# A graph attention kernel: rows without neighbours in two batches, one worked out during the stream

## The chip, the cores and the metric

One core of one Trainium2 chip. The metric is the device time of one execution in microseconds (us), median of three runs, lower is better. The profile comes from one further execution with the hardware profiler. Engines: TensorE (PE), VectorE (DVE), ScalarE (ACT), GpSimd (POOL) and SyncE (SP, which issues DMAs).

## What is computed

```python
N, D = (8192, 128)                       # x: (8192, 128) fp32, adj: (8192, 8192) int32, attn: (256, 1)
h = jnp.maximum(_layernorm(x, axis=-1), 0.0)
s_i = h @ attn[:d]
s_j = h @ attn[d:]
e = jax.nn.leaky_relu(s_i + s_j.T, negative_slope=0.2)
e = e + jnp.where(adj > 0, jnp.float32(0.0), neg_inf)     # neg_inf = -1e9
alpha = jax.nn.softmax(e, axis=1)
return x + alpha @ h
```

Each entry of `adj` is 1 with probability 0.000488, so a row has 4 neighbours on average and 169 of the 8,192 rows have none. In such a row every score has the same -1e9 added, and the softmax goes over all 8,192 columns. At -1e9 fp32 has steps of 64, so for most such rows all scores round to one value and the result is the mean of `h`; where the row's `s_i` is so large that some scores may round to another step (the kernel calls the tile entries "wild"), the whole row has to be worked out.

## The kernel before, in words

Row `64 p + t` lies in partition `p` and tile `t`; there are 64 tiles of 128 rows, taken two at a time as 32 pairs, and each tile is loaded in two halves of 128 x 4096 integers (2 MB).

**Setup.** `x` stays in `x_all`, `h` with its scores in `h_all` (128 x 64 x 132). `h` also goes to a table in DRAM, for gathers.

**Stream**, step `p` of 32. SP loads the halves into the four slots of `adj_ring` (`load_pair`, L352), each as soon as ScalarE has turned the slot's last content into signs (`sign_tile`, L527). TensorE packs the signs of a tile into words that hold column numbers (`pack_tile`, L1147; three buffers `words`), VectorE takes the largest words (`max_tile`, L650), decodes column numbers of up to 8 neighbours per row in 12 slots a pair (`find_pair`, L663) and marks rows with more neighbours than fit (`flag_pair`, L706); TensorE ranks these (`rank_pair`, L1166), VectorE makes one-hot rows of the ranks (`key_pair`, L738), TensorE lists their words (`list_pair`, L1174). GpSimd gathers the neighbours' rows of `h`, 12 indirect DMAs per pair (`gather_pair`, L450). Two steps later VectorE scores them (`score_pair`, L748), ScalarE takes exp (`exp_pair`, L547), VectorE sums 16 weighted rows onto `x` (`add_pair`, L773), and SP stores them. Per segment of 8 pairs the listed ("deep") rows are redone with 16 neighbours: `find_deep`, 17 gathers (`gather_m`, L460), `score_deep`, `add_deep` and an indirect store (`store_m`, L475). Segment 3 is done after the stream.

**Rows without neighbours**, all in the last step (p = 31), in 128 places for the whole matrix. `lone_mark` (L887) finds up to 4 per partition among the 64 tiles; TensorE ranks them (L1210 to L1215); `lone_compact` (L900) makes one-hot rows; TensorE spreads `s_i` and the row numbers over the places (L1217 to L1225); `lone_bounds` (L930) works out ids and maxima; `lone_part` (L946), four parts of 16 tiles, writes the scores of 128 places against 2,048 columns with three instructions of 2,048 elements per partition into slots 2 and 3 of `adj_ring`; ScalarE takes exp (L578 to L581); TensorE multiplies by `h_all` (L1226 to L1231, 128 matmuls); `lone_end` (L961) divides and adds `x`, which GpSimd has gathered (L493 to L498); GpSimd stores (L500 to L504). Behind `lone_part` on VectorE stand `add_pair` and `score_pair` of the last three pairs, then the sizing of the far loop, `score_deep(3)` (L1071), `add_deep(3)` and `lone_end`. GpSimd's order behind the pairs is `store_m(2)`, the gather of x, `gather_m(3)` with 17 gathers, `store_m(3)`, the store of the places.

**Far loop.** Rows that fit nowhere go through a loop over tiles and 32 pieces of 256 columns on all engines. It turns at least once. Rows without neighbours that find no place are such rows (`lost`).

Order between engines is by semaphores: `wait_ge` on an engine holds everything behind it on that engine.

## Time and profile before

| | us |
|---|---|
| median of 3 runs (lowest, highest) | 868.03 (866.70, 868.43) |
| the profiled execution: time | 867.93 |
| the profiled execution: span of the core | 866.2 |
| busy in the span: PE, DVE, ACT, POOL | 460.1, 569.3, 521.1, 571.0 |
| DMA queues moved | 301.56 MB, mean 348 GB/s |
| share of the chain that ended last: DMA, DVE, "issue" | 69%, 11%, 13% |

The span is what the profile shows of the core; 1.7 us lie around it. Busy shares are means over a stream and a tail that have different limits, so a stage has to be read by its own rows. The chain of waits is followed back from the last instruction to whatever released each step. "Idle before" in a timeline is the time an engine stood still before the instruction, with what released it; `issue` means nothing in the profile did. Several VectorE instructions overlap by some 0.1 us, so a group is better timed from its start to the next one's start.

### The profile page before, as it was taken

How to read it: one execution, taken by the hardware profiler on the slowest of the kernel's cores; microseconds unless marked ns; L12 is line 12 of the kernel's file. 1: busy time of each engine (PE TensorE's matmuls, PEld its weight loads, DVE VectorE, ACT ScalarE, POOL GpSimd, SP SyncE). 2: the span in 40 equal slices, each digit the busy share in tenths (PEclk: the TensorE clock that was granted, in tenths of full speed). 3: DMA queues.
4: the chain of work that ended last, by engine and by line, in shares of the span. 5: the costliest groups of instructions: out<-in, count | busy, mean ns of one | idle time of the engine just before them, and what ended most of it. 6: DMA issues, size and time to landing. Idle time of an engine off the chain costs nothing.

```text
span 866.2 us, 7055 instructions
## 1 busy us (share of the span) xinstructions
PE 460.1 (53%) x1605; PEld 191.2 (22%) x1633; DVE 569.3 (66%) x2273; ACT 521.1 (60%) x357; POOL 571.0 (66%) x527
## 2 busy tenths in 40 slices
PE   0665465655555665566555656556566455623601
PEld 0332122221212222122222222222222122213600
DVE  7998266565676666656766465568656566668981
ACT  1895676666676666676666666667666677600200
POOL 6631776666567777666678777667776867758810
PEclk9998777676886678776788686876767788665955
DMA  8799999999999999999999999999999999511000
GB/s 346 286 382 404 399 406 409 410 410 410 406 408 409 410 408 409 405 410 411 404 406 410 408 411 406 414 405 412 404 405 403 408 391 404 196 25 27 18 16 14
DMA packets 39515, 301.56 MB, mean 348 GB/s; under 512 B 10611, under 2 KB 16948, under 8 KB 22065
## 3 DMA queue, kind: packets, MB, share of 16 engines
q1 hardware_dynamic: 24176, 277.23, 79.1%
q0 software_dynamic: 15296, 23.88, 8.0%
q8 instruction: 13, 0.21, 0.1%
q14 instruction: 30, 0.24, 0.1%
HBM read 303.63 MB, written 8.91 MB: 361 GB/s over the span
## 4 chain that ended last, share of the span: by engine, by line
DMA 69%; issue 13%; DVE 11%; ACT 5%; PE 1%; DVEq 0%; POOL 0%; SPq 0%; ACTq 0%; POOLq 0%
DMA adj_ring<-in_adj_dram 68%; ACT sign_ring L533 3%; DVE mixed L797 1%; DVE one_hot L609 1%; ACT h_all L544 1%; DVE adj_ring L954 1%; DVE adj_ring L958 1%; DVE adj_ring L949 1%; DVE mixed_m L879 1%; DMA x_all<-in_x_dram 1%; PE words L1160 0%; DVE codes L616 0%; DVE codes L619 0%; PE words L1220 0%; PE words L1223 0%
## 5 line engine op out<-in xcount | busy, mean ns | idle before, releaser
L533 ACT ACTIVATE sign_ring<-adj_ring,half_neg 128x4096 bf16<-128x4096 int32 x128 | 474.6, 3708 | 226.4 <-DMA adj_ring<-in_adj_dram 226.4
L455 POOL DMA_INDIRECT near<-h_table,near_id x384 | 443.8, 1156 | 198.9 <-issue 109.2
L1160 PE MATMUL words<-sign_ring,pack_w 128*128 128x512 bf16 x1004 | 357.2, 516 | 282.3 <-ACT sign_ring L533 279.6
L656 DVE MAX8 cand<-words 128x8 f32<-128x256 f32 x256 | 91.1, 418 | 223.9 <-PE words L1160 223.8
L1160 PEld LDWEIGHTS words<-sign_ring,pack_w 128*128 128x128 bf16 x1024 | 114.1, 121 | 516.7 <-ACT sign_ring L533 357.2
L797 DVE SCALAR_TENSOR_TENSOR mixed<-near,weight_n,mixed 128x128 f32<-128x128 f32 x448 | 120.3, 345 | 0.0
L470 POOL DMA_INDIRECT near_m<-h_table,id_m x64 | 79.1, 1235 | 19.5 <-issue 19.5
L1152 PE MATMUL words<-place,place_w 128*128 128x512 bf16 x120 | 47.2, 478 | 1.1 <-issue 1.0
L1142 PE MATMUL listing<-h_all 128*1 128x128 f32 x128 | 20.4, 335 | 33.7 <-ACT h_all L544 33.7
L581 ACT ACTIVATE adj_ring<-adj_ring 128x2048 f32<-128x2048 f32 x4 | 7.6, 1910 | 49.8 <-DVE adj_ring L958 49.8
L1179 PEld LDWEIGHTS listing<-cand,one_hot 128*128 128x128 f32 x128 | 28.1, 271 | 12.6 <-issue 6.5
L1229 PE MATMUL words<-h_all,adj_ring 128*128 128x129 f32 x128 | 18.8, 316 | 15.7 <-ACT adj_ring L581 15.7
L1179 PE MATMUL listing<-cand,one_hot 128*128 128x34 f32 x128 | 23.3, 317 | 2.5 <-DVE one_hot L745 2.5
L533 ACT ACTIVATION_READ_ACCUMULATOR sign_ring<-adj_ring,half_neg 128x1 f32 x128 | 23.9, 186 | 0.0
L434 POOL TENSOR_SCALAR h_all<-x_all,codes 128x128 f32<-128x128 f32 x16 | 13.0, 825 | 14.5 <-DVE codes L628 14.5
L1142 PEld LDWEIGHTS listing<-h_all 128*1 128x1 f32 x128 | 12.8, 102 | 41.4 <-issue 27.1
L672 DVE TENSOR_TENSOR codes<-cand_i,code_mask 128x512 int32<-128x512 int32 x32 | 21.9, 684 | 0.0
L1229 PEld LDWEIGHTS words<-h_all,adj_ring 128*128 128x128 f32 x128 | 18.1, 229 | 16.4 <-ACT adj_ring L581 16.4
L642 DVE TENSOR_TENSOR near<-h_all,mixed 128x2048 f32<-128x2048 f32 x8 | 21.5, 2683 | 0.0
L797 DVE SCALAR_TENSOR_TENSOR mixed<-near,weight_n,x_all 128x128 f32<-128x128 f32 x64 | 19.8, 350 | 1.1
L544 ACT ACTIVATE h_all<-x_all,codes 128x128 f32<-128x128 f32 x48 | 18.8, 480 | 0.2 <-DVE codes L628 0.2
L647 DVE TENSOR_REDUCE h_all<-near 128x16 f32<-128x2048 f32 x8 | 18.3, 2288 | 0.3
(213 smaller groups left out, 431.4 us busy)
## 6 DMA issues: line engine op xcount, KB each, us to landing
adj_ring<-in_adj_dram SPq DMA_DIRECT2D x128, 2048.0 KB, 18.9
near<-h_table,near_id POOLq DMA_INDIRECT x384, 6.4
h_table<-h_all POOLq DMA_DIRECT2D x4, 1056.0 KB, 12.2
x_all<-in_x_dram SPq DMA_DIRECT2D x4, 1024.0 KB, 9.6
out_dram<-mixed SPq DMA_DIRECT2D x32, 128.0 KB, 18.5
near_m<-h_table,id_m POOLq DMA_INDIRECT x64, 6.2
adj_ring<-h_table SPq DMA_DIRECT2D x1, 132.0 KB, 3.1
mixed<-in_L_gnn_attn_dram SPq DMA_DIRECT2D x1, 128.0 KB, 6.5
```

Of the source, the lines that this page charges most:

```text
L455: pool.indirect_dma_start(out=near[:, p % RING, k, :], out_offset=None, in_=table, in_offset=bass.IndirectOffsetOnAxis(ap=near_id[:, p % I ...
L470: pool.indirect_dma_start(out=near_m[:, k, :], out_offset=None, in_=table, in_offset=bass.IndirectOffsetOnAxis(ap=id_m[:, k:k + 1], axis=0 ...
L533: nc.scalar.activation(sign_ring[:, n % 4, :], adj_ring[:, n % 4, :], ACT.Sign, bias=half_neg[:, :], accum_out=degree[:, t, h:h + 1]).then ...
L544: nc.scalar.activation(h_all[:, t, 0:D], x_all[:, t, :], ACT.Relu, bias=shift[:, t:t + 1], scale=rstd[:, t:t + 1]).then_inc(h_ready, 1)
L656: last = nc.vector.max(out=cand[:, p % 2, t % 2, 8 * q:8 * q + 8], in_=words[t % 3][:, q * PART:(q + 1) * PART])
L672: nc.vector.tensor_tensor(codes[:, :, :, :].rearrange("p a w c -> p (a w) c"), cand_i[:, :, :].rearrange("p a w -> p (a w)").unsqueeze(2). ...
L797: ins = nc.vector.scalar_tensor_tensor(acc, near[:, e, slot, 0:D], weight_n[:, a * own + k:a * own + k + 1], base, ALU.mult, ALU.add)
L1142: last = nc.tensor.matmul(listing[0:1, 0:D], h_all[:, t, ONE:ONE + 1], h_all[:, t, 0:D], start=(t == 0), stop=(t == TILES - 1))
L1152: nc.tensor.matmul(at[:, k * BANK:(k + 1) * BANK], place_w[:, :], place[:, k * BANK:(k + 1) * BANK], start=True, stop=False)
L1160: last = nc.tensor.matmul(at[:, k * BANK:(k + 1) * BANK], pack_w[:, c, :], sign_ring[:, n % 4, o + k * BANK:o + (k + 1) * BANK], start=Fal ...
L1179: last = nc.tensor.matmul(listing[:, 0:REC], one_hot[:, p % 2, a, :], cand[:, p % 2, a, :], start=(p % SEG == 0 and a == 0), stop=(p % SEG ...
L1229: last = nc.tensor.matmul(lone_sum, lone_p[:, t * P:(t + 1) * P], h_all[:, t, 0:ONE + 1], start=(t == 0), stop=(t == TILES - 1))
```

## The change

The rows without neighbours are taken in two batches. Batch 0 is tiles 0 to 45 (the first 23 pairs), with 64 places; batch 1 is tiles 46 to 63 (the last nine pairs), with 32 places. Each has its own semaphores and buffers; the functions take the batch `b`.

- **Batch 0** runs in the stream, its VectorE steps at the end of a step of the pair loop (`lone_step`): mark in step 22, compaction in 23, bounds and part 0 in 24, parts 1 to 3 in 25 to 27 (each 16 tiles x 64 places), sums of the parts (`lone_add`) in 27 to 30, the end in 30. Its buffers lie in the `x_all` tiles 0 to 39, which `add_pair` has used up. TensorE, ScalarE and GpSimd do their steps in between. TensorE's results lie in the bank `rank`, which `rank_pair` writes too, so `rank_pair` gets waits for VectorE's reads.
- **Batch 1** takes the place of the old code: two parts of 32 tiles x 32 places.
- GpSimd stores batch 0 between `store_m(2)` and the gather of x for batch 1.
- The far loop gets its `x` by a DMA of SP, since `x_all` has been overwritten.
- Unused partitions of the ids are set aside by two more memsets; one more instruction in the bounds drops the ids of a batch that has more rows than places.

```diff
-    LC = 4
-    LT = TILES // LC
+    EARLY = 23
+    FIRST_STEP = EARLY + 1
+    LAST = 1
+    LONE_CAP = (64, 32)
+    LONE_PARTS = (4, 2)
+    LONE_TILES = (slice(0, 2 * EARLY), slice(2 * EARLY, TILES))
+    LONE_BUFS = 3
+    DEAD = 40
...
+        early_x = x_all[:, 0:DEAD, :].rearrange("p t d -> p (t d)")
...
-        lone_p = adj_ring[:, 2:4, :].rearrange("p h w -> p (h w)").bitcast(fp32)
+        lone_p = [[early(lone_size[0], fp32) for _ in range(LONE_BUFS)],
+                  [adj_ring[:, 2, c * lone_size[1]:(c + 1) * lone_size[1]].bitcast(fp32)
+                   for c in range(LONE_PARTS[1])]]
...
-        lone_rank = words[1][:, BANK:BANK + LONE]
-        lone_rec = words[1][:, BANK + 16:BANK + 17]
-        lone_spread = words[0][:, BANK:BANK + P]
-        lone_sum = words[2][:, BANK:BANK + ONE + 1]
+        lone_rank = [rank[:, 72:72 + LONE], words[1][:, BANK:BANK + LONE]]
+        lone_rec = [rank[0:LONE_CAP[0], 76:77], words[1][0:LONE_CAP[1], BANK + 16:BANK + 17]]
+        lone_spread = [rank[:, 448:448 + LONE_CAP[0]], words[0][:, BANK:BANK + LONE_CAP[1]]]
+        lone_sum = [rank[0:LONE_CAP[0], 260:260 + ONE + 1], words[2][0:LONE_CAP[1], BANK:BANK + ONE + 1]]
...
+                    sp.wait_ge(far_free, DC * t + c + 1)
+                    sp.sem_inc(sp_passed, 1)
+                    sp.dma_start(far_x, x_t[:, ds(t, 1), :].rearrange("p o d -> p (o d)")).then_inc(far_x_in, 16)
...
             for p in range(PAIRS):
                 gather_pair(p)
+                if p == FIRST_STEP + 2:
+                    load_lone(0)
...
             store_m(SEGS - 2)
-            pool.wait_ge(lone_id_ready, 1)
-            pool.indirect_dma_start(
-                out=lone_x, out_offset=None, in_=x,
...
+            store_lone(0)
+            load_lone(LAST)
             gather_m(SEGS - 1, range(0, DEEP))
             store_m(SEGS - 1)
...
+            store_lone(LAST)
...
+            def exp_lone(b, c):
+                part = lone_p[b][c % len(lone_p[b])]
+                act.wait_ge(lone_masked[b], c + 1)
+                nc.scalar.activation(part, part, ACT.Exp).then_inc(lone_exp[b], 1)
...
+                if FIRST_STEP <= p - 1 < FIRST_STEP + LONE_PARTS[0]:
+                    exp_lone(0, p - 1 - FIRST_STEP)
...
+            def lone_mark(b):
+                ts = LONE_TILES[b]
+                dve.wait_ge(flags_ready, ts.stop // 2)
                 dve.wait_ge(bounds_ready, 5)
+                if b == 0:
+                    dve.wait_ge(pair_mixed, DEAD // 2)
+                nc.vector.memset(lone_x[b], 0.0).then_inc(lone[b], 1)
+                nc.vector.memset(lone_out[b], 0.0).then_inc(lone[b], 1)
+                nc.vector.memset(lone_id[b], 2 * N).then_inc(lone[b], 1)
...
+            def lone_part(b, c):
+                lt = TILES // LONE_PARTS[b]
+                ts = slice(c * lt, (c + 1) * lt)
+                form = [P, lt, LONE_CAP[b]]
+                part = lone_p[b][c % len(lone_p[b])]
+                tiled = part.rearrange("p (t e) -> p t e", e=LONE_CAP[b])
+                if c >= len(lone_p[b]):
+                    dve.wait_ge(lone_summed[b], c - len(lone_p[b]) + 1)
+                nc.vector.tensor_tensor(tiled, lone_si_b[b].unsqueeze(1).broadcast_to(form),
+                                        h_all[:, ts, SJ].unsqueeze(2).broadcast_to(form), ALU.add) \
+                    .then_inc(lone_masking[b], 1)
...
+            def lone_add(c):
...
+                dve.wait_ge(lone_summed[0], c + 1)
+                if c == 0:
+                    nc.vector.tensor_copy(acc, lone_sum[0]).then_inc(lone[0], 1)
+                else:
+                    dve.wait_ge(lone[0], n + c)
+                    nc.vector.tensor_tensor(acc, acc, lone_sum[0], ALU.add).then_inc(lone[0], 1)
...
+            def lone_step(p):
+                if p == FIRST_STEP - 2:
+                    lone_mark(0)
+                if p == FIRST_STEP - 1:
+                    lone_compact(0)
+                if p == FIRST_STEP:
+                    lone_bounds(0)
+                if 0 <= p - FIRST_STEP < LONE_PARTS[0]:
+                    lone_part(0, p - FIRST_STEP)
+                if 0 <= p - FIRST_STEP - 3 < LONE_PARTS[0]:
+                    lone_add(p - FIRST_STEP - 3)
+                if p == FIRST_STEP + 3 + LONE_PARTS[0] - 1:
+                    lone_end(0)
...
                 if m >= 0 and p % SEG == DEEP_MIX and p < PAIRS - 1:
                     add_deep(m)
+                lone_step(p)
...
-                                                   x_all[:, ds(t, 1), :].rearrange("p o d -> p (o d)"),
+                    dve.wait_ge(far_x_in, 16 * DC * t + 16 * c + 16)
+                    dve.sem_inc(dve_passed, 1)
+                    nc.vector.scalar_tensor_tensor(far_out, far_acc[:, 0:D], far_inv[:, 0:1], far_x,
                                                    ALU.mult, ALU.add).then_inc(far_out_ready, 1)
...
+                if p >= FIRST_STEP - 1:
+                    pe.wait_ge(lone[0], LONE_MARK + LONE_HOT)
+                if p >= FIRST_STEP:
+                    pe.wait_ge(lone_id_ready[0], 1)
+                    pe.wait_ge(lone[0], LONE_MARK + LONE_HOT + LONE_IDS)
+                if 0 <= p - FIRST_STEP - 3 < LONE_PARTS[0]:
+                    pe.wait_ge(lone[0], LONE_MARK + LONE_HOT + LONE_IDS + p - FIRST_STEP - 2)
                 nc.tensor.matmul(place_at, before[:, :], flag[:, e, :], start=True, stop=False)
...
                 list_pair(p - 1)
+                if p == FIRST_STEP - 1:
+                    lone_ranks(0)
+                if p == FIRST_STEP:
+                    lone_spreads(0)
+                c = p - FIRST_STEP - 2
+                if 0 <= c < LONE_PARTS[0]:
+                    lone_matmuls(0, c)
```

`lone_ranks`, `lone_spreads` and `lone_matmuls` are TensorE's old lines (L1210 to L1231) for a batch; a `lone_matmuls(0, c)` is 16 matmuls with 64 places as its weights and a sum of its own, `lone_matmuls(1, c)` is 32 with 32 places.

## Rows read from the trace of the kernel before

**Rows 1.** The page: DMA share in 40 slices, issues of the adjacency with landing.

```profile
DMA  8799999999999999999999999999999999511000
...
adj_ring<-in_adj_dram SPq DMA_DIRECT2D x128, 2048.0 KB, 18.9
```

**Rows 2.** The chain that ended last: start us, us, what.

```profile
736.36 18.88 DMA adj_ring<-in_adj_dram
...
779.93 0.53 DVE adj_ring L905
...
787.41 2.21 DVE adj_ring L949
...
815.42 4.29 DVE mixed L797 x16
...
821.85 4.29 DVE mixed L797 x16
```

**Rows 3.** Groups by line and form, VectorE, 100 to 867 us: count, busy, mean ns.

```profile
L958 DVE SCALAR_TENSOR_TENSOR adj_ring<-adj_ring 128x2048 f32<-128x2048 f32 x4 | 9.2, 2293 | 0.2
...
L905 DVE TENSOR_TENSOR adj_ring<-h_all,adj_ring 128x256 f32<-128x256 f32 x1 | 0.6, 597 | 0.0
...
L763 DVE SCALAR_TENSOR_TENSOR leaky<-valid_score 128x16 f32<-128x16 f32 x32 | 5.7, 178 | 1.1
```

**Rows 4.** Timeline of VectorE, the end: start us, us, instruction, idle before.

```profile
786.20 0.29 DVE L933 COPY adj_ring<-words 128x128 f32<-128x128 f32 x1 [2.92 <-PE words L1223]
...
814.81 0.16 DVE L779 TENSOR_REDUCE total<-weight 128x2 f32<-128x16 f32 x1
...
835.01 0.23 DVE L847 TENSOR_SCALAR score_m<-near_m,si_m 128x16 f32<-128x16 f32 x1
...
847.96 0.17 DVE L1091 TENSOR_SCALAR adj_ring<-adj_ring 128x2 f32<-128x2 f32 x1 [5.90 <-POOLq L511]
...
858.31 0.35 DVE L1128 SCALAR_TENSOR_TENSOR adj_ring<-adj_ring,x_all 128x128 f32<-128x128 f32 x1 [0.24 <-DVE adj_ring L1126]
```

**Rows 5.** Timeline of TensorE, 700 to 867 us.

```profile
782.60 2.07 PE L1220 MATMUL words<-adj_ring 128*128 128x128 f32 x8 [10.83 <-DVE adj_ring L919]
...
810.04 5.48 PE L1229 MATMUL words<-h_all,adj_ring 128*128 128x129 f32 x32 [3.02 <-ACT adj_ring L581]
```

**Rows 6.** Timeline of GpSimd, 700 to 867 us.

```profile
767.69 1.00 POOL L455 DMA_INDIRECT near<-h_table,near_id  x1 [5.39 <-DVE near_id L701]
...
787.15 1.02 POOL L494 DMA_INDIRECT adj_ring<-in_x_dram,adj_ring  x1 [1.23 <-DVE adj_ring L938]
...
788.48 2.01 POOL L465 DMA_INDIRECT x_m<-in_x_dram,row_m  x1 [0.31 <-issue]
...
816.09 1.09 POOL L470 DMA_INDIRECT near_m<-h_table,id_m  x1 [0.30 <-issue]
...
817.48 3.12 POOL L470 DMA_INDIRECT near_m<-h_table,id_m  x1 [0.30 <-issue]
...
823.64 1.01 POOL L470 DMA_INDIRECT near_m<-h_table,id_m  x1 [0.30 <-issue]
```

**Rows 7.** DMA issues of 816 to 832 us and of 842 to 858 us, median landing.

```profile
near_m<-h_table,id_m POOLq DMA_INDIRECT x5, 2.3
...
adj_ring<-in_adj_dram SPq DMA_DIRECT2D x1, 128.0 KB, 6.0
```

**Rows 8.** Busy time per stretch: pair 23, then pair 24.

```profile
578.00:601.00 23.00, 14.21 (x45) 5.46 (x45) 18.27 (x79) 15.51 (x11) 14.48 (x11) 0.73 1.01 410
...
601.00:624.00 23.00, 14.45 (x43) 5.18 (x43) 16.24 (x75) 15.31 (x9) 15.84 (x16) 0.65 1.01 406
```

**Rows 9.** Timeline of VectorE in step 25, then of ScalarE in the same step.

```profile
617.34 1.42 DVE L656 MAX8 cand<-words 128x8 f32<-128x256 f32 x4
...
628.29 0.20 ACT L549 ACTIVATE weight<-below 128x16 f32<-128x16 f32 x1
...
630.34 3.71 ACT L533 ACTIVATE sign_ring<-adj_ring,half_neg 128x4096 bf16<-128x4096 int32 x1 [1.85 <-DMA adj_ring<-in_adj_dram]
```

More of the change, by code:

```diff
@@ new lines, in graph_attention_kernel @@
+        homes = (early, end)
+        widths = [ts.stop - ts.start for ts in LONE_TILES]
+        lost = early(TILES, fp32)
+        lonely = [home(w, fp32) for home, w in zip(homes, widths)]
+        lone_at = [home(w, fp32) for home, w in zip(homes, widths)]
+        lone_top = [home(8, fp32) for home in homes]
+        lone_here = [home(4, bf16) for home in homes]
+        lone_key, lone_si = ([home(LONE, fp32) for home in homes] for _ in range(2))
+        lone_eq, lone_pick = ([home(LONE * w, fp32) for home, w in zip(homes, widths)] for _ in range(2))
@@ L210, in graph_attention_kernel @@
+        lone_x, lone_out = ([home(D, fp32) for home in homes] for _ in range(2))
+        lone_acc = early(ONE + 1, fp32)
+        far_x = end(D, fp32)
+        lone_size = [TILES // n * e for n, e in zip(LONE_PARTS, LONE_CAP)]
+        lone_p = [[early(lone_size[0], fp32) for _ in range(LONE_BUFS)],
+                  [adj_ring[:, 2, c * lone_size[1]:(c + 1) * lone_size[1]].bitcast(fp32)
+                   for c in range(LONE_PARTS[1])]]
+        assert early_taken[0] <= DEAD * D
         far_h = end(DB * COLS, fp32).rearrange("p (k c) -> p k c", k=DB)
@@ L333, in graph_attention_kernel @@
         SIZING = 11
-        LONE_MARK = 4
+        LONE_MARK = 6
         LONE_HOT = 8
-        LONE_IDS = 5
+        LONE_IDS = 6
         FAR_STEPS = 11
@@ L577, in _ @@
             exp_step(PAIRS - 1)
-            for c in range(LC):
-                part = lone_p[:, c * LT * P:(c + 1) * LT * P]
-                act.wait_ge(lone_masked, c + 1)
-                nc.scalar.activation(part, part, ACT.Exp).then_inc(lone_exp, 1)
+            for c in range(LONE_PARTS[LAST]):
+                exp_lone(LAST, c)
             exp_pair(PAIRS - 2)
```

295 lines of the change are left out of this document (161 added, 134 removed).

## The prediction

> **What bounds the kernel now.** I read the page first. For the first 85% of the span the DMA engines are busy in every slice but the first two at 90% or more; in the last 15% they are almost idle [rows 1]. So there are two stages with different limits: a stream in which the adjacency matrix comes in, and a tail of about 110 us after the last half tile. The chain of waits says the same: it goes from load to load up to 755 us, and then through VectorE. The long links of the tail are the masking of the rows without neighbours, from 787.4 to 814.8 us [rows 2, 4]. The timeline of VectorE shows that it waits for almost nothing between 786.2 and 842 us [rows 4]: the tail is a list of VectorE work, and what leaves that list comes off the end, until something else is late. The timeline of GpSimd shows the candidate: it issues 17 gathers (x_m and 16 of near_m) from 788.48 to 824.65 us, and `score_deep(3)` on VectorE at 835.01 needs all of them [rows 4, 6]. The last lands by 825.9 [rows 6, 7]: GpSimd has 9 us to spare there, no more. In the stream, VectorE is busy 18.3 and 16.2 of 23 us in the two fullest steps [rows 8].
>
> **The change, part by part, in the tail.**
>
> Masking. Before: four parts of 16 tiles x 128 places, three instructions of 2,048 elements each, 12 in all, 27.4 us (814.81 - 787.41) [rows 2, 4]. After: two parts of 32 tiles x 32 places, 6 instructions of 1,024. A row of 2,048 takes 2.293 us and one of 16 takes 0.178 [rows 3], so 1.04 ns per element and 1,024 take about 1.23 us; with the overlap seen before (27.4 / 12 = 2.28) the step is 1.22. Six make 7.3 us: **20.1 us less**.
>
> Compaction works on 4 x 18 elements, not 4 x 64. L905 takes 0.597 us for 256 [rows 3]; between it and the 16-element row, 72 elements give about 0.28. Two such and one reduction save some 0.85 us; four one-hot rows of 32 columns, not 128, save about 0.3. Two more memsets add 0.2. TensorE's spreading, for which VectorE waited 2.92 us out of 3.6 [rows 4, 5], has 32 columns or 32 weights, not 128. No row has that shape; between nothing saved and half (1.8 us) I take 1.2, nearer to half, since both operands shrink to a quarter. The bounds have one instruction more and smaller ones: zero, within 0.3. Together 2.2 us. So VectorE's list is **22.3 us** shorter: masking ends at 792.5, and the sizing that ended at 835.0 ends at 812.7.
>
> GpSimd then. Its list before the 17 gathers: `store_m(2)`, which must have ended at 785.9, since 1.23 us of waiting lead up to 787.15; then, new, `store_lone(0)`, whose data has been ready since step 30: 1.02 + 0.30 us. It takes the place of that wait [rows 6], so the `load_lone` comes at 787.5 and x_m at 788.8. Undisturbed, an indirect gather takes 1.00 us and 0.30 to the next: 17 are 22.2 us, or a last start at 809.7. But it isn't undisturbed. While the 2.29 us instructions of the masking run, one gather goes through per VectorE instruction and takes 2.01 us [rows 6]. With instructions of 1.22 us the same lockstep holds for at most the 3 gathers before 792.5: x_m until the step that ends at 789.9, plus 0.9: 1 us lost there and 0.1 to 1 later; I take 1.1. Then the 16 accumulations of a pair, 4.29 us in a row, from 815.42 and from 821.85: a gather that starts 0.67 us into them takes 1.09 us, one 1.79 in takes 1.01, and one 2.06 in takes 3.12 and ends 0.9 after the last of them [rows 2, 6]. Laying the new gathers against the pairs' accumulations (793.1 to 797.4, 799.5 to 803.8, 805.9 to 810.2) one gather in each is held, and costs 0.9, 1.0 and 1.2 us; the short delays before them add some 0.1 each, the lockstep some more where it falls otherwise: 5.7 us in all. The last gather starts at 815.4 and lands 2.3 us later [rows 7]: 817.7. VectorE, ready at 812.7, now **waits about 5 us** for it, where it waited for nothing.
>
> So `score_deep(3)` moves from 835.0 to 817.7, **17.3 us**. What follows it (7 us of deep work, stores, the far loop's one turn) is the same list. New in it: the load of x for the far loop. SP issues it once `far_free` is raised, at which VectorE's own wait ends (847.96), and it is used at 858.31 [rows 4]; the adjacency piece next to it took 6.0 us [rows 7]. It lands 4 us ahead: zero. If that cover were gone, it would cost 6 at most.
> TensorE still runs 128 matmuls for the last batch, four groups like the 5.48 us one [rows 5]: at worst 22 us from 790, done by 812 and needed first for the count of severe rows at 811. What that delays lies under the 5 us wait.
>
> **In the stream.** Batch 0 adds to VectorE: mark 1.1 (seven short instructions, an estimate from the 0.178 us row), compaction 3.4 (2.7 from L905 to where TensorE starts, and four short ones) [rows 2, 5], bounds 1.3 (1.21 before, from 786.20 to 787.41), four parts of 16 x 64 = 1,024 elements with three instructions each, 14.6, sums and end 1.6: 22.0 us in nine steps. Worst are step 23 (18.3 + 3.4 of 23) and step 24 (16.2 + 1.3 + 3.7 of 23) [rows 8]. TensorE, which in `rank_pair` now waits for the end of VectorE's step, not its middle, may lose 7 to 10 us at pairs 23 and 24 (an estimate: the 4.3 us of accumulations and the work added), but it stands idle before each half tile: of each 23 us it is busy 14 [rows 8]. I carry the delay on: `max_tile(50)`, at 617.34 before, comes at 625.4, and the scores of pair 23 end at 628.3. Exactly then ScalarE wants them, at 628.29, and it has 1.85 us before its next half tile [rows 9]. And behind ScalarE stands a second cushion: a load lands 18.9 us after its issue, though 2 MB at 406 GB/s are 5.2 us of transfer [rows 1, 8], so ScalarE may be 13 us late before the DMA engines run dry. The stream costs **nothing** by this; in the range I allow 0 to 3 us. GpSimd is later by up to 5 us in steps 24 to 29 (held gathers, one more load) and has 5.39 us idle before pair 31 [rows 6].
>
> **Sum**: own span 866.2 - 17.3 = 848.9. The profiled execution took 867.93 us in all, 0.1 below the median of 868.03; the sum for that is 850.7, and I say 851.
>
> On the hold of GpSimd the Trainium skill (SBUF — State Buffer, Who interferes with whom) has a rule of its own: a VectorE instruction with two SBUF inputs and a GpSimd instruction that reads SBUF exclude each other, for one whole instruction. The masking rows agree. The 3.12 us row doesn't: the accumulations are some 0.27 us each (4.29 / 16) and it was held for all that were left. By the rule alone the three held gathers would cost 0.3 each, and the gain would be 19 us.
>
> **The rivals.**
> (a) GpSimd isn't late: short instructions let gathers through, and VectorE's list is all. For it: gathers of 1.0 us beside accumulations; 17 at 1.3 land at 812. Against it: a 2.0 to 3.1 us gather in nearly every accumulation. Gain 22.3: **845.7**.
> (b) GpSimd is held far more, with 2.32 us per gather for all 17 as beside the masking: last start 788.8 + 16 x 2.32 = 825.9, landed 828.2, gain 6.8: **861**. Against it: the masking is over by 792.5.
> (c) The other side: the backlog of VectorE reaches the loads. The place is the exp of pair 23 to 26 on ScalarE, queued ahead of the sign of a half tile, whose end lets SP issue the next load. It decides if ScalarE falls more than 13 us behind; then, at worst, all 22.0 us lengthen the stream: 868.0 + 22.0 - 17.3 = **873**, slower. Against it: 628.3 against 628.29, and steps 25 to 30 win time back. A part of it, 3 to 12 us, would give 854 to 863.
> (d) It doesn't do what it says: if more than 64 rows of the first batch, or 32 of the last, need a place, they fall to the far loop, whose single turn lasts some 12 us and which would turn 32 times for every tile: hundreds of us. Counted from the reference's inputs, 41 rows need one of the 64 places and 21 one of the 32, so this is as good as excluded.
>
> **How the numbers follow.** Forecast (GpSimd ends last, 847.5 to 855): 0.68. (a) 0.13. (b) 0.06. (c) in part 0.07, in full 0.04; (d) and the unnamed 0.02. The range 845 to 857 takes in (a), the unknown terms (1.8 us of spreading, 1 to 3 us of lockstep, 0 to 3 us in the stream) and leaves out some 0.15. A difference of 0.2%, 1.7 us, is what can be told from none: faster 0.94, within 0.01, slower 0.05.
>
> **What would show it.** Right: the chain of the end goes through GpSimd's near_m gathers and their landing; VectorE idles 3 to 8 us before `score_deep(3)`; six masking instructions of 1.2 us; gathers of 2 to 3 us only in the accumulations; the last adjacency load lands within 1 us of before. Wrong: no idle there (a), more than 3 us later ends of the stream (c), a wait for `far_x` before the last multiplication, or more than one turn of the far loop (d).

## The result, and the profile after

| | before | after |
|---|---|---|
| median of 4 runs (lowest, highest), us | 867.37 (866.57, 868.43) | 855.60 (854.06, 856.33) |
| the profiled execution: time, span, us | 867.93, 866.2 | 855.79, 854.0 |
| ratio after to before, 95% interval | | 0.9861 [0.9842, 0.9880] |

The change takes 11.8 us off. The forecast was 17; the time lies inside the range. In this document's tables the median counts all executions, while the ratio leaves out slow ones, those more than 1.5% above the fastest of the same kernel; counted in full, `no_batch0` would stand at 0.980 and `reads_first` at 0.989, and the other ratios within 0.003 of what is given.

Between the two profiled spans the difference of 12.2 us splits like this (each piece is the difference of two times in the traces):

| piece | before | after | difference |
|---|---|---|---|
| start to the sign of half tile 114 of 128 | 682.07 | 678.62 | -3.4 |
| from there to the flags of the last pair (L735, L783) | 86.6 | 93.2 | **+6.6** |
| flags to `score_deep(3)` | 66.3 | 47.3 | **-19.0** |
| `score_deep(3)` to the last store's start | 24.5 | 24.5 | 0 |
| last store's start to the end of the span | 6.7 | 10.4 | **+3.7** |

Of the first piece, 2.8 us are there at the first half tile (32.8 us after the start, not 35.6), long before batch 0 starts. In all the traces of this case the first sign starts at 32.8 to 33.0 or at 35.6 to 35.9 us, with batch 0 and without, so this belongs to the execution and not to the change. The two bold plus signs are what the forecast didn't have.

The page of the changed kernel, the slices and the chain (they answer to [rows 1]):

```profile
DMA  8899999999999999999999999999999999911100
GB/s 344 336 379 391 404 408 409 410 411 412 409 411 411 408 409 406 410 410 413 412 408 407 413 409 404 412 410 408 401 405 405 401 363 376 372 35 31 40 22 4
...
DMA 61%; issue 14%; DVE 8%; POOL 6%; PE 5%; ACT 4%; DVEq 0%; SPq 0%; POOLq 0%; ACTq 0%
```

Slices 33 to 35, at 363 to 376 GB/s, were not there before: the DMA engines were no longer fed quite fast enough. And TensorE, 1% of the chain before, now has 5%.

**The tail** did what the forecast said. VectorE's timeline (start, duration, line, tile, idle before; it answers to [rows 4]):

```profile
787.20 0.19 DVE L990 COPY adj_ring<-words 128x32 f32<-128x32 f32 x1 [1.81 <-PE words L1304]
...
788.02 1.22 DVE L1016 TENSOR_TENSOR adj_ring<-adj_ring,h_all 128x1024 f32<-128x1024 f32 x1
789.27 1.22 DVE L1020 SCALAR_TENSOR_TENSOR adj_ring<-adj_ring 128x1024 f32<-128x1024 f32 x1
...
794.25 1.23 DVE L1024 SCALAR_TENSOR_TENSOR adj_ring<-adj_ring 128x1024 f32<-128x1024 f32 x1
795.40 0.16 DVE L827 TENSOR_REDUCE total<-weight 128x2 f32<-128x16 f32 x1
...
815.57 0.15 DVE L1166 TENSOR_SCALAR adj_ring<-adj_ring 128x1 int32<-128x1 f32 x1
819.16 0.23 DVE L895 TENSOR_SCALAR score_m<-near_m,si_m 128x16 f32<-128x16 f32 x1 [3.43 <-DMA near_m<-h_table,id_m]
...
842.45 0.35 DVE L1227 SCALAR_TENSOR_TENSOR adj_ring<-adj_ring 128x128 f32<-128x128 f32 x1 [0.26 <-DVE adj_ring L1223]
```

Six masking instructions take 7.4 us (795.40 - 788.02); they were 27.4. From the flags (771.83) to L1166 VectorE needs 43.7 us, 22.5 less than the 66.2 of before (768.71 to 834.94). Then it waits 3.43 us for a gather. The last multiplication (L1227) waits only 0.26 us, for VectorE itself, so the load of `far_x` costs nothing.

GpSimd's timeline beside it (answers to [rows 6]):

```profile
787.87 1.03 POOL L510 DMA_INDIRECT out_dram<-mixed_m,row_m  x1 [0.30 <-issue]
789.20 1.00 POOL L526 DMA_INDIRECT out_dram<-x_all  x1 [0.30 <-issue]
790.51 1.04 POOL L517 DMA_INDIRECT adj_ring<-in_x_dram,adj_ring  x1 [0.30 <-issue]
791.85 2.01 POOL L496 DMA_INDIRECT x_m<-in_x_dram,row_m  x1 [0.31 <-issue]
794.16 0.99 POOL L501 DMA_INDIRECT near_m<-h_table,id_m  x1 [0.30 <-issue]
...
798.05 3.11 POOL L501 DMA_INDIRECT near_m<-h_table,id_m  x1 [0.30 <-issue]
...
809.29 1.10 POOL L501 DMA_INDIRECT near_m<-h_table,id_m  x1 [0.30 <-issue]
...
812.01 2.06 POOL L501 DMA_INDIRECT near_m<-h_table,id_m  x1 [0.30 <-issue]
...
816.97 0.99 POOL L501 DMA_INDIRECT near_m<-h_table,id_m  x1 [0.31 <-issue]
```

Of the 17 gathers four are longer than 1.01 us (2.01, 3.11, 1.10, 2.06); they lose 4.3 us together. The last starts at 816.97, lands 2.16 later by the chain, and releases L895.

**The stream** is where the forecast failed. TensorE's timeline of the lone matmuls of batch 0 (L1317) and of `rank_pair` (L1276):

```profile
684.27 6.26 PE L1317 MATMUL rank<-h_all,x_all 128*64 128x129 f32 x32 [14.77 <-DVE x_all L1032]
...
709.81 5.46 PE L1317 MATMUL rank<-h_all,x_all 128*64 128x129 f32 x32 [10.98 <-DVE x_all L1035]
...
734.54 5.04 PE L1317 MATMUL rank<-h_all,x_all 128*64 128x129 f32 x32 [10.98 <-DVE x_all L1035]
...
758.86 0.16 PE L1276 MATMUL rank<-flag,before 128*128 128x2 bf16 x1 [6.65 <-DVE x_all L1035]
```

L1032 and L1035 are the two forms of `lone_add`, at the very end of VectorE's step. The code of `lone_matmuls(0, c)` says why: for c > 0 it waits for `lone_add(c - 1)`, because both use the same sums in PSUM. In the order of the instructions TensorE reaches `lone_matmuls(0, c)` in step 26 + c, behind `list_pair`; `lone_add(c - 1)` stands at the end of VectorE's step 26 + c, behind `max_tile(2p+1)`, the finding, the flags and `add_pair`. So TensorE stands still until VectorE's `add_pair` and the work behind it are over, three times, 36.7 us together (14.77 + 10.98 + 10.98), with the next tile's packing queued behind.

How the delay reaches the loads: ScalarE's timeline, its sign of the first half tile after each of these waits:

```profile
692.89 3.71 ACT L576 ACTIVATE sign_ring<-adj_ring,half_neg 128x4096 bf16<-128x4096 int32 x1 [4.12 <-PE words L1258]
...
717.63 3.71 ACT L576 ACTIVATE sign_ring<-adj_ring,half_neg 128x4096 bf16<-128x4096 int32 x1 [6.67 <-PE words L1258]
...
741.95 3.71 ACT L576 ACTIVATE sign_ring<-adj_ring,half_neg 128x4096 bf16<-128x4096 int32 x1 [8.54 <-PE words L1258]
```

ScalarE has no slot to write signs to, because TensorE hasn't packed the old ones; so it frees the slots of the loads later, and SP issues the loads later. The chain of waits goes the same way (start, duration, engine, tile, line):

```profile
705.18 3.84 DVE mixed L845 x15
709.12 0.34 DVE mixed L845
709.81 5.46 PE rank L1317 x32
715.42 0.38 PE words L1250
715.80 3.45 PE words L1258 x16
719.28 0.45 PE words L1250 x2
719.74 3.47 PE words L1258 x16
723.23 1.44 DVE cand L704 x4
```

It is a ring: `add_pair`, lone matmuls, packing, `max_tile`, `add_pair`. From 661.68 us on no load of the adjacency is in the chain; before, the loads went to 755. (From 752 us on the chain follows GpSimd's list. But GpSimd still waited 1.00 us, until 770.80, for VectorE's ids of pair 31, so the last pair still sets where the tail starts.) The windows (busy time of PE, PEld, DVE, ACT and POOL with counts, granted TensorE clock, DMA share, GB/s) show what the DMA engines lose:

```profile
668.00:690.00 22.00, 7.23 (x36) 6.72 (x35) 14.30 (x50) 15.84 (x10) 17.74 (x15) 0.59 1.00 406
690.00:712.00 22.00, 10.86 (x57) 6.61 (x57) 13.80 (x61) 16.15 (x10) 15.05 (x15) 0.80 0.93 365
712.00:734.00 22.00, 11.40 (x64) 7.11 (x63) 13.21 (x60) 15.21 (x9) 13.84 (x13) 0.81 0.96 361
```

VectorE is not overfull there: 13 to 14 of 22 us. Of the 6.6 us, the last sign shows two parts:

```profile
753.85 3.69 ACT L576 ACTIVATE sign_ring<-adj_ring,half_neg 128x4096 bf16<-128x4096 int32 x1
```

It starts at 753.85 (before: 755.26), so the stretch from half tile 114 to it is 75.2 us (753.85 - 678.62) and was 73.2: 2.0 us. They are ScalarE's backlog since its wait that ended at 741.95, not a late load: the last sign has no idle time before it, where it waited 1.42 us for its load before the change, and the last load was issued 54.8 us after the sign of half tile 114 (at 733.43), 54.3 before. From the last sign to the last flags it is 18.0 us and was 13.45: 4.5 us, and in this stretch stands TensorE's wait of 6.65 us in `rank_pair` for the last `lone_add`.

### The profile page after: what moved, and what is told of

It reads as the page before. It is cut to its first block, busy times and chain, and to the rows that moved or that the text cites. A ratio compares the mean times of both kernels' runs of the same rounds, so it can differ in the third digit from the quotient of the medians.

```text
span 854.0 us, 7426 instructions
## 1 busy us (share of the span) xinstructions
PE 456.9 (53%) x1752; PEld 205.0 (24%) x1782; DVE 566.1 (66%) x2314; ACT 519.2 (61%) x359; POOL 563.0 (66%) x529
## 4 chain that ended last, share of the span: by engine, by line
DMA 61%; issue 14%; DVE 8%; POOL 6%; PE 5%; ACT 4%; DVEq 0%; SPq 0%; POOLq 0%; ACTq 0%
DMA adj_ring<-in_adj_dram 60%; POOL near L486 3%; PE words L1258 3%; ACT sign_ring L576 3%; POOL near_m L501 2%; PE rank L1317 2%; DVE mixed L845 1%; DVE one_hot L657 1%; ACT h_all L587 1%; DVE cand L704 1%; DMA x_all<-in_x_dram 1%; DVE mixed_m L927 0%; DVE codes L664 0%; PE words L1250 0%; DVE codes L720 0%
## 5 line engine op out<-in xcount | busy, mean ns | idle before, releaser
L1258 PE MATMUL words<-sign_ring,pack_w 128*128 128x512 bf16 x1003 | 337.6, 496 | 229.0 <-ACT sign_ring L576 226.6
L501 POOL DMA_INDIRECT near_m<-h_table,id_m x64 | 68.3, 1067 | 19.5 <-issue 19.5
L1317 PE MATMUL rank<-h_all,x_all 128*64 128x129 f32 x128 | 21.1, 342 | 36.7 <-DVE x_all L1035 22.0
L1240 PE MATMUL listing<-h_all 128*1 128x128 f32 x128 | 20.2, 333 | 32.0 <-ACT h_all L587 32.0
L1317 PEld LDWEIGHTS rank<-h_all,x_all 128*64 128x64 f32 x128 | 20.2, 181 | 37.1 <-issue 37.0
L1284 PEld LDWEIGHTS listing<-cand,one_hot 128*128 128x128 f32 x128 | 25.2, 246 | 12.1 <-issue 4.9
L1284 PE MATMUL listing<-cand,one_hot 128*128 128x34 f32 x128 | 21.5, 299 | 2.9 <-DVE one_hot L793 2.9
L1276 PE MATMUL rank<-flag,before 128*128 128x2 bf16 x32 | 6.0, 189 | 30.4 <-DVE prior L783 8.2
L611 ACT ACTIVATE adj_ring<-adj_ring 128x1024 f32<-128x1024 f32 x2 | 2.1, 1056 | 31.1 <-DVE adj_ring L1024 31.1
L1317 PE MATMUL words<-h_all,adj_ring 128*32 128x129 f32 x128 | 17.1, 304 | 5.8 <-ACT adj_ring L611 5.8
```

Source lines behind the costliest of these rows:

```text
L501: pool.indirect_dma_start(out=near_m[:, k, :], out_offset=None, in_=table, in_offset=bass.IndirectOffsetOnAxis(ap=id_m[:, k:k + 1], axis=0 ...
L1240: last = nc.tensor.matmul(listing[0:1, 0:D], h_all[:, t, ONE:ONE + 1], h_all[:, t, 0:D], start=(t == 0), stop=(t == TILES - 1))
L1258: last = nc.tensor.matmul(at[:, k * BANK:(k + 1) * BANK], pack_w[:, c, :], sign_ring[:, n % 4, o + k * BANK:o + (k + 1) * BANK], start=Fal ...
L1284: last = nc.tensor.matmul(listing[:, 0:REC], one_hot[:, p % 2, a, :], cand[:, p % 2, a, :], start=(p % SEG == 0 and a == 0), stop=(p % SEG ...
L1317: last = nc.tensor.matmul(lone_sum[b], part[:, k * e:(k + 1) * e], h_all[:, c * lt + k, 0:ONE + 1], start=(first and k == 0), stop=(final ...
```

## The experiments

Four theories for the lost 6.6 us were set against each other. The expectations speak of them.
- **A**: the wait of `lone_matmuls` for `lone_add` of the same step.
- **B**: VectorE's added work as such, 22 us by the forecast's sum.
- **C**: TensorE's 128 added matmuls as such.
- **D**: every wait of TensorE for something at the end of VectorE's step, in `lone_matmuls` and in `rank_pair`.

And for the tail, that the order of GpSimd's list costs some 3 us.

Four sets of runs follow. The kernel before took 876 to 897 us in them and not 867, so times are compared by their ratio to the kernel before in the same set; the kernel with the change was measured again in the second. The record has one chip number for sets 1, 2 and 4 and another for set 3.

**First set** (the kernel before: 897.13). `later` takes the lone matmuls one step later, so that `lone_add(c - 1)` is long done:

```diff
-                c = p - FIRST_STEP - 2
+                c = p - FIRST_STEP - 3
                 if 0 <= c < LONE_PARTS[0]:
                     lone_matmuls(0, c)
```

> One number: TensorE's lone_matmuls(0, c) is put one step of the pair loop later (c = p - 27, not p - 26), everything else as in the changed kernel. Theory A (TensorE stands before lone_matmuls(0, 1) to (0, 3) until VectorE has done lone_add of the part before, at the very end of the same step; with nothing packed meanwhile, ScalarE and then the loads wait): by then lone_add is long done, the three waits of 15, 11 and 11 us vanish, ScalarE never waits for TensorE, the flags of pair 31 come about 6.6 us earlier after half tile 114 than in the changed kernel, median about 849 (855.6 less 6.6). Rival B (VectorE's 22 us of added work in steps 22 to 30 delay the stream through the exp on ScalarE): the work is unchanged, so the time is too, 855 to 856. Rival C (TensorE's 5.5 us of added matmuls per step fill it up): also unchanged, 855 to 856.

`pool_order` puts the gathers of segment 3 ahead:

```diff
             store_m(SEGS - 2)
+            gather_m(SEGS - 1, range(0, DEEP))
             store_lone(0)
             load_lone(LAST)
-            gather_m(SEGS - 1, range(0, DEEP))
```

> The changed kernel with GpSimd's store of batch 0 and the gather of x for batch 1 moved behind the 17 gathers of segment 3; the stream is not touched. Theory (the last gather of near_m sets the end of the tail, VectorE idles 3.4 us for it): the gathers start 2.6 us earlier, VectorE's idle time before score_deep(3) shrinks from 3.4 to 0.8 us, median 2.6 lower, about 853. Rival (GpSimd's gathers are held by VectorE's instructions wherever they fall, so that they end at the same time): idle time stays near 3.4, median unchanged at 855.6.

`both` has both edits.

> Both edits together: later matmuls of batch 0 and GpSimd's new order. If the two losses are independent, 6.6 and 2.6 us add up: median about 846.4. If one hides the other (the stream's end shifts GpSimd's list against VectorE's and the gathers are held elsewhere), it is nearer to 849.

`no_batch0` leaves batch 0 out altogether: none of its steps on any engine, no wait for it in `rank_pair`. Its rows are not worked out, and the far loop's sizing leaves out `lost`, so what is timed is the tail with 32 places and a stream like that of before.

```diff
-                lone_step(p)
...
-                if p >= FIRST_STEP - 1:
-                    pe.wait_ge(lone[0], LONE_MARK + LONE_HOT)
...
-                c = p - FIRST_STEP - 2
-                if 0 <= c < LONE_PARTS[0]:
-                    lone_matmuls(0, c)
```

> Leaves out all of batch 0 (its 41 rows keep the value that the stream gives them): batch 1 alone with its 32 places, so the tail of the changed kernel with the stream of the kernel before. Theory A: the stream loses nothing (6.6 us less than the changed kernel after half tile 114), and GpSimd's list is one store shorter (1.3 us): about 847.7. If the later-matmul kernel and this one agree within 1.5 us, batch 0 costs the stream nothing but by that wait; if this one is 3 us or more lower than it, batch 0's work costs the stream something of its own. The 3.7 us between the last store and the end of the span, longer than before (10.4 against 6.7), are looked for here too: gone if batch 0's code brings them.

| | us | ratio to before, 95% |
|---|---|---|
| later | 901.15 | 1.0070 [1.0034, 1.0106] |
| pool_order | 908.59 | 1.0109 [1.0072, 1.0147] |
| both | 905.67 | 1.0096 [1.0062, 1.0131] |
| no_batch0 | 878.80 | 0.9734 [0.9687, 0.9782] |

Only `no_batch0` is faster than before. All that has batch 0 is slower, so something costs more here than in the first measurement, and `later`, for which theory A expected 849, doesn't remove it. The change itself was not in this set; it is in the next.

**Second set** (before: 894.05): the change, `later`, `both` and `no_batch0`, unchanged.

> The changed kernel itself once more, beside the kernel before and the three others of this call on one chip, since the first four ran on a chip where the kernel before takes 897 us and not 867. If this chip is like the first one: 855 to 856, and TensorE's three long waits before lone_matmuls. If it is like the second: the ratio to before lies above 1.

> lone_matmuls(0, c) one step later, as in the run later. Theory A (the three waits on TensorE): on a chip where before takes 867 us, about 849, 6.6 us under the changed kernel of this call, and ScalarE waits for no TensorE instruction. Rivals B and C (the added work on VectorE or TensorE as such): no different from the changed kernel.

> Later matmuls and the 17 gathers ahead of the store of batch 0 and of the gather of x. If GpSimd's last gather sets the end of the tail: VectorE's idle time before score_deep(3) falls from about 3.4 to under 1 us, about 846.4. If not, it equals the run with the later matmuls.

> Leaves out batch 0 altogether. Theory A: its stream equals that of the later-matmul kernel within 1.5 us, and its tail is one store (1.3 us) shorter: about 847.7. If it is 3 us or more under the later-matmul kernel, batch 0's work costs the stream something beside the three waits.

| | us | ratio to before, 95% |
|---|---|---|
| after_again | 906.95 | 1.0118 [1.0067, 1.0170] |
| later_again | 903.45 | 1.0117 [1.0079, 1.0156] |
| both_again | 903.48 | 1.0124 [1.0090, 1.0158] |
| no_batch0_again | 877.69 | 0.9813 [0.9781, 0.9846] |

**Here the change is 1.2% slower than before**, where it was 1.4% faster in the first measurement. The traces show one thing that differs: VectorE pauses in the stream for microseconds with no releaser that a profile can name. VectorE's timeline of `after_again` and of `no_batch0_again`:

```profile
531.30 0.18 DVE L808 SCALAR_TENSOR_TENSOR valid_score<-invalid,score 128x16 f32<-128x16 f32 x1 [8.91 <-issue]
...
598.44 0.18 DVE L808 SCALAR_TENSOR_TENSOR valid_score<-invalid,score 128x16 f32<-128x16 f32 x1 [8.51 <-remote]
```

```profile
535.96 0.18 DVE L802 SCALAR_TENSOR_TENSOR valid_score<-invalid,score 128x16 f32<-128x16 f32 x1 [6.80 <-remote]
...
592.82 0.18 DVE L802 SCALAR_TENSOR_TENSOR valid_score<-invalid,score 128x16 f32<-128x16 f32 x1 [6.47 <-remote]
```

They are there with batch 0 and without, also before it starts. The accumulations of `add_pair` show it too, as a group of VectorE (busy, mean ns, idle before); first the changed kernel in the first measurement, then in this set:

```profile
L845 DVE SCALAR_TENSOR_TENSOR mixed<-near,weight_n,mixed 128x128 f32<-128x128 f32 x448 | 120.3, 346 | 0.0
```

```profile
L845 DVE SCALAR_TENSOR_TENSOR mixed<-near,weight_n,mixed 128x128 f32<-128x128 f32 x448 | 126.3, 349 | 38.5 <-DVE mixed L845 23.3 <-issue 10.8 <-remote 3.4
```

In the first measurement these 448 instructions had 0.0 us of idle time between them; here 38.5. `no_batch0_again` has 49.5 and is faster than before all the same, so the pauses alone don't make the change slow. The reading offered here is that they use up VectorE's slack, so that what makes TensorE wait for the end of VectorE's step now counts; that is argued, not shown. The page's chain has VectorE at 30% and the DMA engines at 25%, where the first measurement had 8% and 61%.

TensorE's waits from 570 to 780 us (line, waited for, us in total, times, longest), `after_again`:

```profile
PE rank L1317 <- DVE x_all L1035: 21.1, 2, 10.5
PE rank L1317 <- DVE x_all L1032: 17.6, 1, 17.6
...
PE rank L1276 <- DVE x_all L983: 11.0, 1, 11.0
PE rank L1276 <- DVE x_all L1006: 9.4, 1, 9.4
```

and `later_again`:

```profile
PE rank L1276 <- DVE x_all L1035: 20.2, 2, 16.2
...
PE rank L1276 <- DVE x_all L1006: 8.0, 1, 8.0
PE rank L1276 <- DVE x_all L983: 7.7, 1, 7.7
```

So the edit of `later` did what it was to do: L1317 waits for VectorE no more. But `rank_pair` (L1276), which writes the same bank, waits for the same `lone_add` in the next instructions of TensorE's order. The wait moved from one line to the other, and the ratio stayed: 1.0117 beside 1.0118. A is too narrow for this place; D names both. B and C are still open.

**Third set** (before: 888.99). `reads_first` keeps all work of batch 0 and `later`, and takes those VectorE steps that TensorE waits for (compaction, bounds, `lone_add`, the end) ahead of `add_pair`; mark and parts stay behind it:

```diff
+            def lone_reads(p):
                 if p == FIRST_STEP - 1:
...
+                lone_reads(p)
                 for g in mixes:
...
-                c = p - FIRST_STEP - 2
+                c = p - FIRST_STEP - 3
```

> Batch 0 complete, its matmuls one step later as in the run later, and VectorE's compaction, bounds, sums and end of batch 0, which read the bank rank, put ahead of add_pair in their step; the parts stay behind it. So rank_pair on TensorE, which has to wait for these reads, waits some 5 us less in steps 23, 24 and 27 to 30. Theory D (on this chip the stream loses by TensorE standing in rank_pair for the end of VectorE's step, and VectorE, which has little slack here, then standing for TensorE): most of the loss of the stream goes, the median falls from 903 to 907 to within 8 us of the kernel without batch 0 (878), so to 878 to 890. Rival B (VectorE's added work as such): no different from the later-matmul kernel, about 903. On a chip where before takes 867 us, theory A gives 849 for it.

`busy_vector` is `no_batch0` with 12 instructions like the masking ones, of 1,024 elements, at the ends of steps 24 to 27, on buffers that nobody reads, so that no other engine waits for them. Batch 0's rows are again not worked out.

```diff
+                    nc.vector.tensor_tensor(tiled, h_all[:, 0:64, SI].unsqueeze(1).broadcast_to(form),
+                                            h_all[:, 0:16, SJ].unsqueeze(2).broadcast_to(form), ALU.add) \
+                        .then_inc(lone_masking[0], 1)
...
```

> Leaves out batch 0 and puts in its place, on VectorE alone, the twelve instructions of 1,024 elements of its four parts (3.7 us at the end of each of steps 24 to 27, written to the dead part of x_all); no other engine has work or waits from it. Rival B (VectorE's work as such): 14.6 us of the loss or more come back over the kernel without batch 0: 878 + 15 = 893 or more. Theory D (the waits between TensorE and VectorE): within 4 us of the kernel without batch 0, 878 to 882. On a chip where before takes 867 us both give what the kernel without batch 0 gives.

`places64` has no batch 0 either, but works out everything: one batch over all 64 tiles at the end, with 64 places, four parts of 1,024 elements.

```diff
-    LONE_CAP = (64, 32)
-    LONE_PARTS = (4, 2)
-    LONE_TILES = (slice(0, 2 * EARLY), slice(2 * EARLY, TILES))
+    LONE_CAP = (64, 64)
+    LONE_PARTS = (4, 4)
+    LONE_TILES = (slice(0, 2 * EARLY), slice(0, TILES))
...
-                lone_step(p)
```

> No batch in the stream: one batch at the end for all 64 tiles, as in the kernel before, with 64 places in place of 128 (62 rows need one) and four parts of 16 tiles x 64. VectorE's twelve instructions take 1.22 us, not 2.28: 12.7 us less masking, about 0.8 less around it. If the tail's gain carries over whole and nothing else is touched: 13.5 us under the kernel before on any chip (854 where before takes 867, about 881 where it takes 894), with VectorE not waiting for the last gather (it has 9 us to spare there before, and the gathers are held less). If GpSimd sets the end after all, a wait of up to 4 us at score_deep(3) and 9 to 10 us of gain.

| | us | ratio to before, 95% |
|---|---|---|
| reads_first | 879.34 | 0.9843 [0.9791, 0.9894] |
| busy_vector | 872.69 | 0.9820 [0.9783, 0.9858] |
| places64 | 873.71 | 0.9817 [0.9775, 0.9858] |

**B falls.** `busy_vector` stands at 0.9820 beside `places64` at 0.9817 in the same set (and `no_batch0_again` at 0.9813 in another). Its added work is more than the 14.6 us expected: eight of its twelve instructions read 64 entries of `h_all` that lie 132 elements apart and took 1.97 to 2.02 us each, the other four 1.22 to 1.23, 20.9 us in all. That is nearly all of batch 0's 22 us of VectorE work, and with nobody waiting for it, it cost nothing that shows.

**C and D are not settled by this set.** By the ratios D is right: `reads_first` stands at 0.984, where `later_again`, with the same matmuls in the same steps, stands at 1.012, and the two kernels differ only in the place of VectorE's reads. But neither the change nor `later` ran in this set, on this chip, and the traces bear the ratios out only in part. TensorE's waits in `reads_first` from 570 to 780 us; L1279 is `rank_pair` there and L1287 is `list_pair`:

```profile
PE listing L1287 <- DVE one_hot L793: 60.7, 8, 14.1
...
PE rank L1279 <- DVE x_all L1035: 5.0, 1, 5.0
PE rank L1279 <- DVE x_all L983: 2.7, 1, 2.7
```

In `rank_pair` TensorE waits 7.7 us for batch 0, where `later_again` had 35.9 (20.2 + 8.0 + 7.7). But it waits 60.7 us for VectorE one function later, in `list_pair`, where `later_again` had 8.0, `later` 24.6 and `busy_vector` 26.2. And VectorE stands 22.5 us (6.07 + 6.25 + 10.13) before `lone_add`, which now comes ahead of `add_pair` and by the code waits for TensorE's matmuls (the profile names no releaser there). The stretch of the stream in which batch 0 runs, from the sign of half tile 88 (the first of step 22) to the flags of the last pair:

| traces | us |
|---|---|
| first measurement: before, the change | 234.1, 240.0 |
| sets 1 and 2: `after_again`, `pool_order`, `later`, `both`, `both_again`, `later_again` | 265.3, 262.9, 263.6, 266.3, 259.8, 253.9 |
| sets 1 and 2, no batch 0: `no_batch0`, `no_batch0_again` | 240.4, 249.4 |
| set 3: `reads_first` | 253.8 |
| set 3, no batch 0: `busy_vector`, `places64` | 239.3, 238.3 |

In its trace `reads_first` is no shorter there than `later_again`, and 14.5 us longer than `busy_vector` beside it. (The traced executions of `later` and `later_again` were the fastest of theirs, 8 to 10 us under the median; the other four with batch 0 are 6 to 12.5 us longer than `reads_first`.) What batch 0 costs in the stream where VectorE pauses, and by which wait, stays open.

**Fourth set** (before: 875.79). `reads_first_pool` is `reads_first` with the order of `pool_order` on GpSimd.

> The kernel of the run reads_first with GpSimd's 17 gathers ahead of the store of batch 0 and the gather of x for batch 1. If the last gather sets the end of the tail: VectorE's wait of 3.4 us before score_deep(3) falls to under 1, the ratio to before goes from 0.984 to about 0.981. If something else does (pauses in the tail that no engine explains on these chips): no wait, and a ratio that stays at 0.984 within the interval.

It took 860.23 us (858.04 to 861.53), ratio 0.9822 [0.9794, 0.9850]. Its profile, of 857.1 us, has none of the pauses (0.0 us between the 448 accumulations), though the record has the chip number of sets 1 and 2 for it, so its stages can be laid beside the first traces. TensorE's timeline, windows, and VectorE's timeline:

```profile
704.19 4.27 PE L1320 MATMUL rank<-h_all,x_all 128*64 128x129 f32 x32
...
726.24 3.73 PE L1320 MATMUL rank<-h_all,x_all 128*64 128x129 f32 x32
```

```profile
690.00:740.00 50.00, 29.91 (x147) 16.67 (x148) 33.59 (x140) 34.95 (x20) 35.56 (x32) 0.86 1.01 392
```

```profile
822.47 0.23 DVE L895 TENSOR_SCALAR score_m<-near_m,si_m 128x16 f32<-128x16 f32 x1 [0.83 <-DMA near_m<-h_table,id_m]
```

The lone matmuls wait for nothing, the DMA share from 690 to 740 us is full, and from half tile 114 to the last flags it is 87.4 us: before 86.6, with the change 93.2. **The stream's loss is gone**, 5.8 of 6.6 us; from half tile 88 on it is 236.1 us, beside 234.1 before and 240.0 with the change. This kernel has all of batch 0's work on VectorE and all 128 matmuls on TensorE, so B and C fall for the 6.6 us of the first measurement, and only who waits for whom is left. Whether the later matmuls (A) would have done it without the earlier reads (D) isn't shown, since `later` never ran without the pauses. At `score_deep(3)` VectorE waits 0.83 us in place of 3.43, and flags to `score_deep(3)` is 44.8 us in place of 47.3: the order on GpSimd is worth 2.6 us in the trace. In the medians it isn't seen: 0.9822 beside 0.9843 from another set, `both_again` 1.0124 beside `later_again` 1.0117 in the same one, and `pool_order` and `both` no faster than `later` in the first. In `pool_order`, `both` and `both_again` VectorE doesn't wait at `score_deep(3)` either (`later_again`: 6.05 us), yet flags to `score_deep(3)` is 59.5 us in `both_again` and 58.6 in `later_again`; the order gave nothing there.

**Which version is best?** `places64` and `reads_first_pool` stand at 0.982, each in its own set, where the change stands at 1.012 in a third. `places64` is 15.3 us under the kernel before (13.5 were expected), and VectorE has no wait before `score_deep(3)`, as expected; `reads_first_pool` is 15.6 us under it. Between the two no difference is shown. `places64` is the simpler: it gets its gain from half the places alone and leaves the stream as it was. Neither was run where the kernel before takes 867 us; there the change stands at 0.9861, and that the two would be better there too is argued from the 5.8 and 2.6 us above, not shown.

**The end of the span.** From the start of the last store (L559, before L516) to the end of the span it is 10.38 us in the changed kernel and 6.71 before. It sorts the kernels cleanly: all eight further runs with batch 0 have 10.41 to 10.47, all four without it 6.74 to 6.80. The last store is the same instruction with the same operands. In all nine profiles with batch 0 one packet of the instruction queue q14 falls in the last 16 us, as here in the DMA view of the changed kernel from 830 us on, and in none of the five without it:

```profile
q14 instruction: 1, 0.01, 0.1%
```

That goes together; that the one causes the other is not shown. What the traces do show is that 3.7 us of this change's time lie behind the start of its last store.

## Why the prediction was right or wrong

- **Masking, compaction, spreading: 22.3 us.** Right: 22.5. Masking 7.4 us against 7.3 forecast; the spreading's wait 1.81 us against the 2.92 of before, 1.1 saved where 1.2 was taken.
- **GpSimd ends last, VectorE waits 5 us.** Right in kind; it waits 3.43. The held gathers lost 4.3 us, not 5.7 (of which the named terms make 4.5, and the rest was put on the lockstep without a row): beside the 1.22 us instructions only that of `x_m` was held, and of the three pairs' accumulations the middle one (802.43 to 806.77) held none, where 0.9 to 1.2 us were laid to each. So the tail gives 19.0 us, 1.7 more than the 17.3. On this the Trainium skill (SBUF — State Buffer, Who interferes with whom) says that a gather is kept out for one whole instruction of VectorE. The 2.01 us gather beside the masking agrees; the 3.11 us one, beside instructions of 0.27 us each, doesn't. By that rule the gain would have been about 19 us. It was 19.0, but for another reason: two gathers were held longer than the rule has it, and others, started in the middle of accumulations, not at all.
- **`far_x`: zero.** Right, L1227 waits for nothing but VectorE.
- **"The stream costs nothing by this".** Wrong, and this is the step that failed: a term put at nothing, with 0 to 3 us allowed, that measured 6.6. The text went through VectorE's work per step and through `rank_pair`'s waits, 7 to 10 us at pairs 23 and 24. Those waits came out at 7.8 and 7.7 and did no harm. But it never asked what `lone_matmuls` waits for. Its wait for `lone_add` is at the end of the same VectorE step, so the delay doesn't come once or twice and get absorbed; it closes a ring, 10.98 to 14.77 us in three steps running and 6.65 in a fourth. Price: 6.6 us, 2.0 of it at the last sign and 4.5 behind it. `reads_first_pool`, with the same work and those waits gone, has 0.8 of the 6.6.
- **Rival (c)**, a part of it (3 to 12 us in the stream, 854 to 863 in all, chance 0.07), is what came, by the forecast's own sign too (the stream ends more than 3 us later). It had the size and the wrong place. It looked at exp of pair 23 on ScalarE at 628 us, where nothing waited. The backlog came through `words`, the signs' slots and ScalarE's waits of 4 to 9 us at 690 to 742 us. The loads were held up less still: of 36.7 us that TensorE stood still, 2.0 reached the last sign and 0.5 the issue of the last load.
- **GpSimd's 5.39 us before pair 31** were to take up its delay. They did, with 1.00 us to spare: pair 30's gathers started at 752.53, not 744.99, since the ring made VectorE late with their ids.
- **The end of the span: +3.7 us** was in no rival.
- The 2.8 us that the profiled execution of the change was ahead at its first half tile hide part of this. By its own steps the sum would be -19.0 + 6.6 + 3.7 = -8.7; the trace's -12.2 has 3.4 from the piece up to half tile 114. Whether the executions without a profile had this lead too isn't known.
- **The number.** That the time came out inside the range is in part luck: 1.7 us more gain in the tail and the 3.4 us lead stand against 6.6 and 3.7 us that weren't forecast.
- The chance of 0.05 for slower was too small in a way the traces of before couldn't show: with the kernel before at 894 us, the change is slower.

## What to carry to other kernels

When work is woven into a pipelined loop, list for each in-order engine what every new wait waits for and where in the *other* engine's step that stands: a wait for the end of the same step closes a ring however idle both engines look, and moving one wait can hand it on to the next user of the same PSUM bank (from L1317 to L1276 here). Putting what others wait for at the front of the step, and work for which nobody waits at its end, is the version that lost nothing where VectorE doesn't pause; check with a trace where the waits went, on all engines. Before weaving at all, price the plain version: fewer places alone stood at the same ratio as the best version with two batches.

## What the runs showed that wasn't expected

- The same two kernels differ by -1.4% in one measurement and by +1.2% in another, where VectorE pauses (38.5 us between 448 accumulations, 0.0 in the first). Leaving batch 0 out was faster in both sets in which that was run (0.9734, 0.9813). What the pauses are stays open. They may not belong to a chip: sets 2 and 4 have the same chip number on record, and the trace of set 4 has none.
- 3.7 us more behind the start of the last store in each of nine traces with batch 0 and in none of the five without.
- The same VectorE instruction of 1,024 elements took 1.22 us in `lone_part` and 1.97 to 2.02 us in `busy_vector`. The operand that runs along the 64 places lies closely packed in the first and 132 elements apart in the second.
- Which gather is held can't be told from where it starts. One that starts 2.1 us into a pair's accumulations (798.05) took 3.11 us and one 3.1 us in (812.01) took 2.06, both ending 0.9 us after the last accumulation; beside the middle pair's, three starting 0.3, 1.6 and 2.9 us in took 1.00 each.
- Not tried: `rank_pair` without its waits for batch 0. What those waits still cost in `reads_first` is open. So is `later` alone where the kernel before takes 867 us (there A might be enough), and the change or `later` beside `reads_first` in one set.
